# Padded DRAM rows for the convolution windows, extra products in the lead, a bound from raw inputs, and new instruction orders

## What is computed

```python
# 1. conditional mixing: a small MLP and a softmax give 8 shares per sample
att = softmax(gelu(gelu(c @ W0 + b0) @ W1 + b1) @ W2 + b2)         # (32, 8)
z = einsum('boi,bih->boh', einsum('bk,koi->boi', att, weight), x) + (att @ bias_k)[:, :, None]
# 2. attention with sign weights: 32 query heads, 8 key/value heads of 16; a head sees 32 tokens
y = nan_to_num(z @ sign(w).T * (mean|w| * scale))                  # for q, k, v and the output
x = x + attention(z)
# 3. grouped convolution over the 512 features (9 taps, 4 groups of 8 tokens) plus a condition term
v = conv1d(x, weight, padding=4, groups=4) + (c @ c_weight.T + bias)[:, :, None]
# 4. low-rank experts: 8 experts of rank 16, the best two by a router, softmax of their logits
x = x + sum over experts of gate * ((v @ A_e.T) @ Bm_e.T) * 0.5
```

## Time and profile before

| | us |
|---|---|
| median of 3 runs | 136.77 (136.05 to 140.3) |
| the profiled execution | 136.54 |
| its span, first to last instruction | 134.7 |
| TensorE busy | 114.7 |
| VectorE busy | 93.9 |
| ScalarE busy | 63.6 |
| GpSimd busy | 48.1 |

### The profile page before, as it was taken

The page is one execution under the profiler, slowest core; times in us unless marked ns, Lnnn a source line. Parts: engine busy times, 40 slices in busy tenths (PEclk is TensorE's granted clock), DMA queues, the critical chain, the costliest instruction groups (busy, mean ns, idle before and its releaser), DMA issues. The chain is left out here.

```text
span 134.7 us, 2543 instructions
## 1 busy us (share of the span) xinstructions
PE 114.7 (85%) x876; PEld 89.4 (66%) x876; DVE 93.9 (70%) x251; ACT 63.6 (47%) x139; POOL 48.1 (36%) x58
## 2 busy tenths in 40 slices
PE   1389999695799997899799999999999669967970
PEld 1269699694697996698698876767676329543720
DVE  0073999629795987999588797797456555395862
ACT  4629889964233688362637355364331202230320
POOL 1117000001605693366579989674330030000000
PEclk9999999999779999999999999999999995999999
DMA  3999999500000000001852924919392949496123
GB/s 65 276 363 421 400 412 409 215 6 2 0 5 0 0 0 0 5 2 78 158 80 90 211 88 100 208 53 221 120 207 67 216 127 208 134 223 242 78 100 133
DMA packets 18317, 19.27 MB, mean 143 GB/s; under 512 B 960, under 2 KB 14080, under 8 KB 17920
## 3 DMA queue, kind: packets, MB, share of 16 engines
q1 hardware_dynamic: 18304, 19.11, 51.6%
HBM read 14.91 MB, written 4.19 MB: 142 GB/s over the span
## 5 line engine op out<-in xcount | busy, mean ns | idle before, releaser
L360 POOL TENSOR_TENSOR probs<-probs,row_inv 128x512 f32<-128x512 f32 x16 | 16.7, 1049 | 17.2 <-DVE row_inv L864 17.2
L1216 PE MATMUL bank<-mixed_hi,qkv_sign 128*128 128x256 f32 x72 | 18.1, 293 | 1.2 <-DVE scale_v L746 1.2
L1217 PE MATMUL bank<-mixed_lo,qkv_sign 128*128 128x256 f32 x72 | 17.3, 282 | 0.0
L366 POOL TENSOR_TENSOR x_all<-x_all,o_out 128x512 f32<-128x512 f32 x8 | 10.2, 1278 | 13.8 <-DVE o_out L878 13.8
L1216 PEld LDWEIGHTS bank<-mixed_hi,qkv_sign 128*128 128x128 f32 x72 | 14.0, 194 | 1.5 <-DVE scale_v L746 1.3
L1294 PE MATMUL bank<-wo_sign,attn_hi 128*128 128x512 f32 x32 | 13.4, 418 | 1.3 <-DVE attn_lo L869 1.3
L1217 PEld LDWEIGHTS bank<-mixed_lo,qkv_sign 128*128 128x128 f32 x72 | 13.9, 194 | 0.0
L507 ACT ACTIVATE probsT<-bank 128x512 f32<-128x512 f32 x16 | 9.6, 597 | 7.7 <-PE bank L1270 7.5
L501 ACT ACTIVATE probs<-probs 128x512 f32<-128x512 f32 x16 | 9.9, 628 | 6.9 <-DVE probs L854 6.9
L1294 PE MATMUL bank<-wo_sign,attn_lo 128*128 128x512 f32 x32 | 12.6, 393 | 0.0
L1258 PE MATMUL bank<-keys_diag,queries 64*128 64x128 f32 x128 | 9.5, 288 | 3.6 <-issue 2.6
(11 more groups left out here) (141 smaller groups left out, 232.1 us busy)
## 6 DMA issues: line engine op xcount, KB each, us to landing
rows_sb<-x_turned SPq DMA_DIRECT2D x24, 256.0 KB, 4.5
x_all<-in_x_rows SPq DMA_DIRECT2D x4, 512.0 KB, 9.3
x_turned<-x_all SPq DMA_DIRECT2D x8, 256.0 KB, 4.9
out_rows<-x_all SPq DMA_DIRECT2D x8, 256.0 KB, 2.6
qkvT_sb<-in_qkvT SPq DMA_DIRECT2D x4, 384.0 KB, 6.4
rows_sb<-in_qkv_rows SPq DMA_DIRECT2D x1, 1536.0 KB, 10.5
rows_sb<-in_wo_rows SPq DMA_DIRECT2D x1, 1024.0 KB, 13.3
woT_sb<-in_woT SPq DMA_DIRECT2D x1, 1024.0 KB, 15.8
```

The source lines that it names most:

```text
L360: pool.tensor_tensor(probs[:, t % 2, h, :, :], probs[:, t % 2, h, :, :], row_inv[:, t % 2, h, :].unsqueeze(2).to_broadcast([P, HALF, TOKENS]),
L366: pool.tensor_tensor(x1[:, t, :], x_all[:, t, :], o_out[:, t % 2, :], ALU.add).then_inc(x1_ready, 1)
L1216: mm(dst, w, mixed_hi[:, ph, cols(i % 2, PAIR)], start=(ph == 0 and n % 2 == 0), stop=False)
L1217: last = mm(dst, w, mixed_lo[:, ph, cols(i % 2, PAIR)], start=False, stop=(ph == PHASES - 1 and n % 2 == 1))
```

## The change

- **Windows.** Tile t is written to one of two internal DRAM tensors, `win_rows`, as 512 runs of 512 bytes, each into a run of 130 elements with a pad at both ends. A read of one shift is then one row of 2080 elements (8320 bytes) for each of 32 partitions, starting `shift` elements further on. `clear_pads` on SP writes zeros over both tensors beforehand, from buffers that `clear_windows` has now zeroed whole on 32 partitions; it moves from the head of POOL's list to behind `spread_keys(3)`. `windowed` is one semaphore per buffer.
- **TensorE in the lead.** `keep_busy(n)` issues n products of 128 by 128 ones into a bank that nobody reads: 4 before the first layer product, 1 after each of the first two, 4 before `spread_shares`, 2 before `mix_bias_first`.
- **Loads.** The second and third piece of `cond_sb` are one transfer.
- **The bound** comes from the sums of |mix_w|, |mix_b| and |shares|, taken on DVE before and between the mixing steps, and has one factor more.
- **Tile 7's residual** moves from POOL to DVE (`residual_last`).
- **Later bias products later; new orders.** The lists of TensorE, DVE, ACT and POOL are reordered. On TensorE among others: `mix(1, 0)` ahead of `project_first(mixed_hi, 0)`, `turn_scale_v` and `total_bound` earlier, `mix(2, 1)` ahead of `project(1, 0)`, `gather_conv` earlier, `convolve(0)` behind `score(7)`. On ACT `sum_x(0)` goes first and the copies of the bias products 1 and 2 go behind `high_part(0, 0)`.

The core of the diff:

```diff
-        x1_dram = nc.dram_tensor("x1_turned", (ROWS, HIDDEN), F32, kind="Internal").ap()
+
+        win_rows = [nc.dram_tensor(f"x1_rows{n}", (TOKENS * win_w + 2,), F32, kind="Internal").ap() for n in range(2)]
...
-            sp.dma_start(cond_sb[:, first:layers], cond_pack[:, first:layers]).then_inc(in_layers, 16)
-            sp.dma_start(cond_sb[:, layers:], cond_pack[:, layers:]).then_inc(in_own, 16)
+            sp.dma_start(cond_sb[:, first:], cond_pack[:, first:]).then_inc(in_layers, 16)
...
+            def clear_pads():
+                sp.wait_ge(win_cleared, 2)
+                for n in range(2):
+                    sp.dma_start(win_rows[n][0:TOKENS * win_w].rearrange("(p w) -> p w", w=win_w),
+                                 x1_win[n][0:TOKENS].rearrange("p s g m -> p (s g m)")).then_inc(pads_cleared, 16)
+                    sp.dma_start(win_rows[n][TOKENS * win_w:].rearrange("(p w) -> p w", p=1),
+                                 x1_win[n][0:1, 0, 0, 0:2]).then_inc(pads_cleared, 16)
+                sp.wait_ge(pads_cleared, 64)
+
             def to_window(t):
-                rows = x1_dram[t * P:(t + 1) * P, :]
-                sp.wait_ge(x1_ready, t + 1)
-                sp.dma_start(rows, x1[:, t, :]).then_inc(x1_stored, 16)
+                rows = win_rows[t % 2]
+                runs = rows[0:TOKENS * win_w].rearrange("(cp sg m) -> sg cp m", cp=TOKENS, m=STEPS + 2)
+                if t < TILES - 1:
+                    sp.wait_ge(x1_ready, t + 1)
+                else:
+                    sp.wait_ge(x1_last_ready, 1)
+                reached(sp, windowed[t % 2], 48 * (t // 2))
+                sp.dma_start(runs[:, :, 1:1 + STEPS], x1[:, t, :]).then_inc(x1_stored, 16)
                 sp.wait_ge(x1_stored, 16 * (t + 1))
-                if t == 0:
-                    sp.wait_ge(win_cleared, 4)
                 reached(sp, conv_done, t - 1)
                 for shift in range(3):
-                    sp.dma_start(x1_win[t % 2][TOKENS * shift:TOKENS * (shift + 1), :, :, 2 - shift:2 - shift + STEPS]
-                                 .rearrange("p s g m -> p (s g) m"),
-                                 rows.rearrange("(sg c) (ph m) -> (c ph) sg m", c=MEMBERS_IN, m=STEPS)
-                                 ).then_inc(windowed, 16)
+                    sp.dma_start(x1_win[t % 2][TOKENS * shift:TOKENS * (shift + 1), :, :, :].rearrange("p s g m -> p (s g m)"),
+                                 rows[shift:shift + TOKENS * win_w].rearrange("(p w) -> p w", w=win_w)).then_inc(windowed[t % 2], 16)
...
+            clear_pads()
...
                 for n in range(2):
-                    pool.memset(x1_win[n][0:TOKENS, :, :, 1:2], 0.0).then_inc(win_cleared, 1)
-                    pool.wait_ge(win_cleared, 2 * n + 1)
-                    pool.memset(x1_win[n][2 * TOKENS:WINDOW, :, :, STEPS:STEPS + 1], 0.0).then_inc(win_cleared, 1)
-                    pool.wait_ge(win_cleared, 2 * n + 2)
-
-            clear_windows()
+                    pool.memset(x1_win[n][0:TOKENS, :, :, :], 0.0).then_inc(win_cleared, 1)
+
             spread_keys(0)
             spread_keys(1)
             normalise(0, 0)
+            spread_values(0)
+            normalise(0, 1)
             spread_keys(2)
+            normalise(1, 0)
             spread_keys(3)
-            normalise(0, 1)
-            normalise(1, 0)
-            spread_values(0)
+            clear_windows()
...
+            sum_x(0)
             turn_shares()
             sign_qkv(0)
             sign_qkv(1)
+            spread_mix_bias(0)
+            sign_qkv(2)
+            sign_qkv(3)
             keep_conv_bias()
-            spread_mix_bias(0)
-            sum_x(0)
-            sign_qkv(2)
             high_part(0, 0)
-            sign_qkv(3)
+            spread_mix_bias(1)
+            spread_mix_bias(2)
             sum_x(1)
-            spread_mix_bias(1)
             high_part(0, 1)
+            high_part(1, 0)
             sum_rows(0, 0)
...
+            def sum_mix_inputs():
+                dve.wait_ge(in_mix_w, 16)
                 dve.wait_ge(sums_cleared, 1)
-                dve.wait_ge(outer_b_ready, 2)
-                v.tensor_reduce(sums[:, PAIRS:PAIRS + 1], agg[:, :, :].rearrange("p t o -> p (t o)"), AX_X, ALU.add,
+                v.tensor_reduce(sums[:, PAIRS:PAIRS + 1], mix_w_sb[:, :, :].rearrange("p o k -> p (o k)"), AX_X, ALU.add,
                                 apply_absolute_value=True).then_inc(sums_ready, 1)
-                v.tensor_reduce(sums[0:TILES * MIXES, PAIRS + 1:PAIRS + 2], outer_b.rearrange("p t q o -> p (t q o)"), AX_X,
+                dve.wait_ge(in_mix_b, 16)
+                v.tensor_reduce(sums[0:TILES * MIXES, PAIRS + 1:PAIRS + 2], mix_b_sb[:, :, :].rearrange("p t o -> p (t o)"), AX_X,
                                 ALU.add, apply_absolute_value=True).then_inc(sums_ready, 1)
+
+            def sum_shares():
+                dve.wait_ge(att_kept, 1)
+                v.tensor_reduce(sums[:, PAIRS + 2:PAIRS + 3], att_sb[:, :], AX_X, ALU.add,
+                                apply_absolute_value=True).then_inc(sums_ready, 1)
+
+            def sum_scales():
...
+            def residual_last():
+                t = TILES - 1
+                dve.wait_ge(y_scaled, t + 1)
+                v.tensor_tensor(x1[:, t, :], x_all[:, t, :], o_out[:, t % 2, :], ALU.add).then_inc(x1_last_ready, 1)
...
+            def keep_busy(n):
+                for _ in range(n):
+                    mm(bank[7][:, 0:P], ones[:, :], ones[:, :], start=True, stop=True)
...
             mix_bias_rest()
+            mix(1, 0)
             project_first(mixed_hi, 0)
-            mix(1, 0)
             mix(1, 1)
             project_first(mixed_lo, 0)
             project_first(mixed_hi, 1)
+            turn_scale_v()
             mix(2, 0)
             project_first(mixed_lo, 1, (0, 1))
+            mix(2, 1)
             project_first(mixed_lo, 1, (2, 3))
+            total_bound()
             project_first(mixed_lo, 1, (4, 5))
-            turn_scale_v()
             project(1, 0)
-            total_bound()
             project(1, 1)
-            mix(2, 1)
             mix(3, 0)
             score(0)
-            mix(3, 1)
             project(1, 2)
             spread_o_scale()
+            mix(3, 1)
             score(1)
...
             project_out(3)
+            turn_probs(5, 0)
             attend(4)
-            turn_probs(5, 0)
+            score(7)
             convolve(0)
             turn_probs(5, 1)
-            score(7)
             project_out(4)
             turn_conv(0)
```

More of the change, by code:

```diff
@@ L109, in build @@
         table_load = sb("table_load", [P, 2])
-        sums = sb("sums", [P, PAIRS + 3])
+        sums = sb("sums", [P, PAIRS + 4])
         bound = sb("bound", [1, PAIRS + 12])
@@ L246, in _ @@
         def _(sp):
-            first, layers = COND["b0"].stop, COND["b2"].stop
+            first = COND["b0"].stop
             def load_pair(i):
@@ L775, in sum_magnitudes @@
+            def sum_scales():
                 dve.wait_ge(scale_ready, 1)
-                v.tensor_reduce(sums[:, PAIRS + 2:PAIRS + 3], scale_all[:, 0:BLOCKS], AX_X, ALU.add,
+                v.tensor_reduce(sums[:, PAIRS + 3:PAIRS + 4], scale_all[:, 0:BLOCKS], AX_X, ALU.add,
                                 apply_absolute_value=True).then_inc(sums_ready, 1)
             def bound_qkv():
-                by_agg, by_bias, by_scale = (bound[:, n:n + 1] for n in range(PAIRS, PAIRS + 3))
+                by_w, by_b, by_share, by_scale = (bound[:, n:n + 1] for n in range(PAIRS, PAIRS + 4))
@@ L1161, in mix_bias_first @@
             def mix_bias_first():
+                keep_busy(2)
                 pe.wait_ge(outer_b_ready, 1)
@@ L1228, in total_bound @@
                 pe.wait_ge(aggb_ready, 3)
-                pe.wait_ge(sums_ready, 3)
+                pe.wait_ge(sums_ready, 4)
                 pe.wait_ge(x_sums, PAIRS)
-                mm(ps_bound[0:1, 0:PAIRS + 3], ones[:, 0:1], sums[:, :], start=True, stop=True).then_inc(bound_done, 1)
+                mm(ps_bound[0:1, 0:PAIRS + 4], ones[:, 0:1], sums[:, :], start=True, stop=True).then_inc(bound_done, 1)
             def spread_o_scale():
```

315 lines of the change are left out of this document (161 added, 154 removed).

## The result

The changed kernel takes 160.12 us (median of 4 runs, 159.12 to 160.85), the kernel before 136.41 (136.04 to 140.3) beside it. The ratio is 1.174, with a 95% interval of 1.164 to 1.185: 23.7 us slower, where 131.9 us was forecast.

What follows compares the result with a forecast made beforehand. TensorE was taken to bound until 106.7 us, with transfers setting the pace from about 82 us. Span 134.7 - 5.1 (lead) + 1.1 (ring start) - 0.6 (turns) = 130.1, plus 1.84 = 131.9 us; own range 128.5 to 134, overall 125 to 137.

Steps and rivals of the forecast that it cites:

- The bound ... its one more step costs about 0.2 us, hidden: Lead, DVE: the new bound's extra step costs about 0.2 us, covered by `project(1, 0)` and `project(1, 1)`.
- so I take 28: 0.2 us more: Write of a tile as 512-byte runs: 28 ns a packet, so 0.2 us more than the plain write.
- The rival of the slow write: Padded write to DRAM: unaligned runs take far longer than 28 ns a packet, total 146.9 us; chance 0.09.
- The reads: Three window reads per tile: limited by their 32 destination partitions, 3.9 us instead of 4.2, a gain of 0.3 us a turn.
- starts 1.1 us later in the order: Ring of writes and reads on SP: starts 1.1 us later because `convolve(0)` now comes after `score(7)`.
- Part 1: TensorE in the lead: constant products raise the clock by 9 us, so the mixing runs faster; net gain 1.8 us.
- the lower bound: Lead, the other bound of the constant products' effect: the clock does not rise, nothing is gained, and 1.4 us are lost.
- Part 2: Lead up to `score(0)`: earlier scale and later clearing gain 0.3, 2.6 (idle) and 1.7 us (clock), less 1.3 for memsets.
- The wait for `scale_v`: TensorE before `project(1, 0)`: of 1.2 us of waiting, 0.3 us taken as gained (0 to 1.2).
- The 1.3 us for the memsets: POOL: longer clearing memsets take 3.7 us and delay the softmax of tile 1; 1.3 us charged (0 to 3.7).
- The sum of the lead: All terms of the lead: 1.8 + 0.3 + 2.6 + 1.7 - 1.3 = 5.1 us gained.
- What would show it: Signs to check; outright failure if TensorE idles anew between 40 and 80 us, for `normalise(1, 1)` or the softmax feeding `score(7)`.

Runs made afterwards that it cites:

- the kernel with long rows and no products: The changed kernel without the share factor in its bound and without the constant products: 139.87 us, ratio 1.018 to the kernel before.
- the kernel with short rows: The changed kernel without the share factor in its bound, windows as in the kernel before: 132.68 us with the constant products, 132.61 without.

## Why the prediction was wrong, by its own steps

- **"The bound ... its one more step costs about 0.2 us, hidden".** This is the step that failed, by 20 us. I priced the bound's instructions and not its value. The kernel branches on that value, and no row of the trace of before could show a path that isn't taken; the rule of the branch and the inputs could. The case was in none of the rivals.
- **The write, "so I take 28: 0.2 us more".** Mis-sized: 1.85 us. The price of a packet was near (35 ns, 0.4 us more for the tile than the plain write's (0.22 + 0.99 + 0.14) x 8 = 10.8 us of engine time, 0.67 us each). Not in the sum were the start, 0.4 us later, the engines not all being busy from first to last packet (0.6 us longer instead of 0.4), and the time from the last packet to the reads, 0.8 us longer. The rival of the slow write had the right place and sign with 0.09, but looked for it in the packets too.
- **The reads.** A gain of 0.3 us a turn was forecast, at 203 GB/s. In three full windows of 1 us in the ring (82 to 85 us of the kernel with long rows and no products) they ran at 216, 208 and 200 GB/s. Reads and write together keep their 5.9 us, so what the reads gained the longer packets' time behind them took back. A turn grew by 1.0 us, the wait behind the last packet. That the length of a packet doesn't bind the reads is borne out; that the 32 partitions do is not shown, since the run that was to test it was held by something else.
- **The ring "starts 1.1 us later in the order".** Didn't happen. With short rows, `convolve(0)` moved from 80.65 to 73.42 us, and the ring was let go by the residual of tile 2 instead: its write leaves at 74.86, its reads at 77.41.
- **Part 1, +1.8.** Nothing was gained. The condition, a clock that has risen by 9 us, was met neither with the products nor without (13.7 us was the earliest rise). The products and the joined load did put off the mixing by 1.3 to 1.4 us, as the lower bound had it, but the time moved by less than 1 us.
- **Part 2.** `score(0)` near 30 us was right only where the clock rose early (29.93 us without the products, 30.80 with them, both with short rows). In the changed kernel, where the rise came at 23.9 us, it stood at 35.35, later than the 34.62 before. The idle time of 2.6 us and the clock behind it were right. The wait for `scale_v`, of which 0.3 us was taken as gained, went whole: in the kernel with short rows TensorE doesn't wait for it at all. The 1.3 us for the memsets were nothing. The sum of the lead, 5.1 us, came out close, and that was luck: the kernel with short rows gained 4.6 us against 137.3 beside it, though 1.8 us of mine were never there, and 1.3 were charged for nothing.
- **What would show it.** "TensorE idle anew between 40 and 80 us" was named as the sign of failure, and it came, but for VectorE's instructions and not for `normalise(1, 1)`.

In one line: 136.4, minus 4 to 5 for the lead and the orders, plus 7.9 for the long rows, plus 20 for the branch, gives 160.

## What to carry to other kernels

Where a kernel branches on a bound, an edit of the bound is priced by its value against the threshold, on the real inputs, before its instructions are; a looser bound can be a valid one and still cost 20 us of 140. A write that others wait for is priced from its issue to the issue of what waits for it, in a row that has the same run length and pitch, because here the packets' own time (0.67 against 1.1 us) was a quarter of the 1.85 us. And in a ring of write, landing and reads on one queue, ask first whether the next write can go ahead of the reads: that order brought 6.7 us where new layouts brought a loss.

## What the runs showed of the hardware

- The same tile of 256 KB, written from SBUF to DRAM with nothing beside it, took 2.08 us to the next issue as 128 rows of 2 KB, 3.07 us as 512 runs of 512 bytes at a pitch of 512, 3.20 at 576 and 3.93 at 520.
- Of these 512 runs, first to last packet took 1.44 to 1.46 us at each pitch. The time from the last packet to the waiting issue was 0.36 us at a pitch of 512 bytes, 0.48 at 576 and 1.21 at 520.
- In the lead TensorE worked at the 1.2 GHz level until some time between 13.7 and 23.9 us, differently in kernels with the same lead and whether or not constant products came first. The column of the granted clock says 1.00 there, ahead of the trace's first record of it.
- A transfer whose source has an outermost dimension of 3 kept about 3 of the 16 DMA engines busy (share 0.20) and moved 59 to 62 GB/s.
